# Two of four rounds per chunk weighted by ScalarE instead of VectorE in the four-head graph-attention layers

## The reference

```python
h = (h_in @ W).reshape(n, Hh, Cc)                # Hh = 4 heads, Cc = 64
alpha_s = jnp.sum(h * a_s, axis=-1)
alpha_d = jnp.sum(h * a_d, axis=-1)
e = jax.nn.leaky_relu(alpha_s[src] + alpha_d[dst], 0.2)
m = jax.lax.stop_gradient(jax.ops.segment_max(e, dst, num_segments=n))
ex = jnp.exp(e - m[dst])
alpha = ex / jax.ops.segment_sum(ex, dst, num_segments=n)[dst]
out = jax.ops.segment_sum(h[src] * alpha[:, :, None], dst, num_segments=n)
return out.reshape(n, Hh * Cc) + b
```

## Time and profile before

| What | us |
|---|---|
| Device time, median of 3 runs | 5079.66 |
| lowest and highest of the 3 | 5040.54, 5084.57 |
| Span of the profiled execution (first to last instruction) | 4873.4 |
| Around the span: the three runs less the span | 167 to 211, by the median 206.3 |
| Gathers of the first GAT layer, first start to last start | 3149.6 to about 3795 |
| Gathers of the second GAT layer | 3878.8 to 4526.0 |

### The profile page before, as it was taken

One profiled execution on the slowest core, in us unless ns is written; L12 is line 12 of the kernel. 1 busy time (PEld: TensorE's weight loads), 2 busy tenths in 40 slices (PEclk: granted clock), 3 DMA queues, 4 the chain that ended last, 5 costly groups with the idle time before them and its releaser, 6 DMA issues. The chain is left out here.

```text
span 4873.4 us, 62986 instructions
## 1 busy us (share of the span) xinstructions
PE 3036.0 (62%) x14559; PEld 2055.8 (42%) x14560; DVE 2601.7 (53%) x6219; ACT 1386.5 (28%) x3757; POOL 1985.7 (41%) x1861
## 2 busy tenths in 40 slices
PE   5498655597646455553669993355555455555289
PEld 3255113354213333332358993243333333343267
DVE  6655988655974678874331111344444444444421
ACT  0311431212421577773114441110110210110134
POOL 0000430001421777775002224377777477777300
PEclk9999875555777666776559996677776677767579
DMA  0132000222013677764012222244444244444200
GB/s 19 60 96 86 0 5 16 81 93 69 0 59 126 180 188 196 197 191 133 6 47 83 80 71 68 72 101 100 101 101 100 63 101 100 101 100 100 71 18 21
DMA packets 269152, 413.89 MB, mean 85 GB/s; under 512 B 98337, under 2 KB 192053, under 8 KB 268721
## 3 DMA queue, kind: packets, MB, share of 16 engines
q0 software_dynamic: 98256, 295.59, 23.1%
q1 hardware_dynamic: 169124, 116.08, 7.9%
q10 hardware_dynamic: 1728, 1.72, 0.1%
HBM read 373.41 MB, written 39.84 MB: 85 GB/s over the span
## 5 line engine op out<-in xcount | busy, mean ns | idle before, releaser
L1098 PE MATMUL gt_part<-gt_wv,all_ident 128*128 128x260 f32 x1920 | 733.3, 548 | 651.3 <-DVE gt_wv L1001 651.3
L918 POOL DMA_INDIRECT gt_rows<-h_rows,gt_idx x960 | 1003.3, 1045 | 314.6 <-issue 300.1
L1098 PEld LDWEIGHTS gt_part<-gt_wv,all_ident 128*128 128x128 f32 x1920 | 497.2, 271 | 887.5 <-DVE gt_wv L1001 786.3
L1098 PE MATMUL att_part<-att_wv,all_ident 128*128 128x264 f32 x960 | 386.1, 571 | 331.5 <-ACT att_wv L1080 210.0
L918 POOL DMA_INDIRECT att_rows<-kv_rows,att_idx x480 | 512.8, 1068 | 148.6 <-issue 145.0
L1098 PEld LDWEIGHTS att_part<-att_wv,all_ident 128*128 128x128 f32 x960 | 258.3, 282 | 459.5 <-DVE att_wv L1001 315.0
L1080 ACT ACTIVATE att_wv<-att_rows,att_wv 128x32 f32<-128x32 f32 x1920 | 419.9, 308 | 3.9
L1075 ACT ACTIVATE gt_wv<-gt_score 128x20 f32<-128x20 f32 x240 | 57.1, 238 | 1218.9 <-DVE gt_score L995 1218.9
L974 DVE TENSOR_TENSOR gt_prod<-gt_rows,gat_own 128x16 f32<-128x16 f32 x240 | 42.2, 176 | 574.8 <-SPq L896 551.2
L1001 DVE TENSOR_TENSOR gt_wv<-gt_rows,gt_wv 128x1024 f32<-128x1024 f32 x240 | 292.5, 1219 | 0.4 <-ACT gt_wv L1075 0.4
L608 POOL TENSOR_TENSOR ixcd_off_p<-ixcd_lane_e,all_iota_h 128x2048 f16<-128x2048 f16 x26 | 96.4, 3709 | 413.4 <-issue 304.7
(11 more groups left out here) (455 smaller groups left out, 5680.9 us busy)
## 6 DMA issues: line engine op xcount, KB each, us to landing
ixbs_parts_bc<-key_parts_s SPq DMA_DIRECT2D x28, 1024.0 KB, 6.2
ixbd_parts_bc<-key_parts_d SPq DMA_DIRECT2D x28, 1024.0 KB, 6.3
ex_w<-in_W SPq DMA_DIRECT2D x16, 1024.0 KB, 7.4
gt_rows<-h_rows,gt_idx POOLq DMA_INDIRECT x960, 2.9
att_rows<-kv_rows,att_idx POOLq DMA_INDIRECT x480, 3.8
y_rows<-ex_y POOLq DMA_DIRECT2D x55, 128.0 KB, 2.0
kv_rows<-qv_kv_all SPq DMA_DIRECT2D x5, 1300.0 KB, 6.5
gt_idx<-neighbours_d SPq DMA_DIRECT2D x240, 2.0 KB
```

The costliest lines, as they stand in the source:

```text
L918: pool.indirect_dma_start(out=rows[:, k, r, :], out_offset=None, in_=table, in_offset=bass.IndirectOffsetOnAxis(ap=idx[:, k, r:r + 1], axi ...
L1098: last = pe.matmul(part[:, k, 0:h * av], c.ident[:, :], wv[:, k, r, :, :].rearrange("p h f -> p (h f)"), start=(r == 0), stop=(r == ROUNDS ...
```

## The change

The number of rounds that ACT weights was half of the four in the eight-head layer and none in the GAT layers. It is now half in all three calls.

```diff
@@ attend, L848
-    act_rounds = ROUNDS // 2 if qk else 0
+    act_rounds = ROUNDS // 2
     dve_rounds = ROUNDS - act_rounds
```

## The result

| | Kernel before | Changed kernel |
|---|---|---|
| Device time, median | 5082.11 us (4 runs, 5040.54 to 5087.62) | 5137.28 us (4 runs, 5127.67 to 5143.28) |
| Ratio after / before | | 1.0119, 95% interval 1.008 to 1.0158 |
| Span of the profiled execution | 4873.4 us | 5141.7 us |

The change costs 1.2%; I had forecast 1.4% the other way. The span of the changed kernel stands 1.6 us under the time of its own run (5143.28), so next to nothing lies around a span. The 206 us that I had put "around the span" of the kernel before were inside the executions that were timed: its trace came from an execution of some 4875 us, the like of which none of the timed ones was.

The account below looks back on a forecast made before the run. POOL's gather issue was taken to bound the two GAT layers; 92.3 us of stretching gone less 23 back gains 69, so 5079.7 - 69 = 5010.7 us, with 8 in 10 between 4970 and 5052.

Parts of the forecast that it names:

- around the span: Time outside the profiled span, 206 us, taken as untouched, so the gain was subtracted from the median of timed runs.
- What bounds the kernel: In both GAT layers POOL's gather issue sets the pace, 5.01 us a chunk, stretched to 5.37 by L1001.
- The port rule: L1001 holds gathers 0.13 us after their start; halved to 0.68 us, it brings their mean from 1.045 to 0.97.
- The sum: Both GAT layers: 92.3 us of stretching gone, 23 back, 69 gained; span 4804, time 5010.7 us, 1.4% faster.
- the term for L1009: In GAT chunks k = 2 and 3, L1009 moves up and holds 65 of 120 gathers: 17 us back.
- So it stays hidden: The register load behind L1001 would still run under the shorter L1001 of 0.68 us.
- ACT under cover: ACT's eight activations, 2.2 us a GAT chunk, end 1.5 us before DVE's half and cost nothing in the loop.
- B: Rival: no change, 5080 us; stretched gathers only show another limit, such as the DMA engines; chance 0.13.
- C: Rival: ACT becomes the bound in the GAT layers, POOL waiting on it; 29 us more, 5109 us; chance 0.03.

Follow-up runs that it names:

- e11: The changed kernel again, its half written another way (same instructions), against the kernel before on a pausing machine: 5139.96 us, ratio 1.0132.
- e2: Kernel before with DVE weighting two of four GAT rounds and nobody the other two, quiet machine: 4804.16 us, ratio 0.9847.
- e3: Kernel before plus eight unused ACT activations per GAT chunk, DVE still weighting all four rounds, quiet machine: 4876.91 us, ratio 0.9998.
- e5: The changed kernel again, its half written another way (same instructions), against the kernel before on a quiet machine: 4793.54 us, ratio 0.983.
- e7: Changed kernel with ACT weighting three of four GAT rounds and DVE one: 5014.41 us in one run, kernel before 5085.53.
- e16: Changed kernel with ACT weighting three of four GAT rounds, measured again on a pausing machine: 5075.96 us, ratio 0.9946 to the kernel before.
- e19: Changed kernel plus a POOL fill of 128 columns ahead of each GAT chunk's third gather, pausing machine: 5172.28 us, ratio 1.0111 to the kernel before.

## Why the prediction was wrong

- **What bounds the kernel: wrong for the machine that was measured, and the step that failed.** "So the pace is set by how fast POOL issues gathers" holds for the execution that was profiled, and for no timed one. The evidence stood in the table: a span of 4873.4 beside runs of 5040 to 5085. I wrote "What lies around it is untouched, so against the median of the runs 5079.7 - 69", and took 206 us, 4% of the kernel, for overhead around a span without asking. After it, time and span differ by some 2 us in every run. What the runs showed in its place: the pauses take 200 us of the kernel before, POOL stands for slots, and what the port gives back (70 us, e11) is lost again in POOL's pauses (129 us more), by pauses that grow and by ACT's lost cover.
- **The port rule: right.** The gathers' mean was to be 0.97 us: 0.960 quiet, 0.968 and 0.969 pausing. L1001 took 0.684 (0.68 forecast). e2 gains by it alone.
- **The sum, on the machine that the trace came from: right, and 12 us short.** 69 forecast, 81 measured. Most of the difference is the term for L1009: 17 us forecast, 5.4 counted, since for k = 2 it starts 0.83 us after the start of L1001 and not 0.68, behind a register load that the shorter L1001 no longer hides. "So it stays hidden" was wrong there, to the good. For k = 0 and 1 L1009 did not move at all: it starts 1.5 to 1.6 us after the start of L1001 in both kernels, where no gather is near. L1001 itself kept 7.8 us, where I had 4.
- **ACT under cover: right on a quiet machine** (e3: 0.9998), wrong on a pausing one, where POOL waits 245 us for L1080 [e11]. "DVE stays the later of the two" and "The cover is 1.5 us" took for granted that DVE stands for the rows of the next chunk. It does in e5, and the cover is 1.5 us there; where POOL has run ahead the rows are there, and ACT ends 0.8 us behind DVE [e11].
- **Rivals.** B (no change, 5080) and C (ACT in POOL's way) each had a part of it: POOL's idle time does name ACT, as C's sign was to be, though an activation costs 0.25 us and not 0.60. None had pauses in it.

Open: what the pauses are, whether faster gathers cause their growth, and why three rounds on ACT have fewer of them than the even split. They occur in the three stretches with continuous gathers, not elsewhere, and in some jobs only. That the split with three rounds waits less is measured, in e7 and e16; its reason is not. Every run here has a recorded span, so none shows whether the pauses would be there without recording. Single runs lie some 40 us under the others in either condition (4836 beside 4873, 5035 beside 5081), also without a known reason.

## What to carry to other kernels

Before reading one row, hold the profiled span against the timed runs: where they are 4% apart, the trace shows an execution of another kind, and a bound read from it needs room for the engines that it shows idle. A faster bounding engine is worth only the slack behind it. The cover of an engine that works beside another is to be worked out once more for the case that the other does not wait. Of a split between engines try every ratio: three of four rounds on ACT beats the kernel before in both conditions (0.9849 and 0.9946), the even split in one only.

## What the runs showed of the hardware that I had not expected

- The instruction streams of SP and DVE, and in the eight-head layer that of ACT, can fall to about one instruction in 1.4 us (a register move of 29 ns took up to 1,387), in some jobs and not in others on the same chip; 200 us in 5,080 here. In the traces this comes only with continuous gathers of POOL, and is over within some 3 us of the last one.
- A gather issued by POOL is held by a DVE operation on two SBUF operands only if that started about 0.025 us or more ahead of the gather and still runs 0.13 us after the gather's start. The gather then ends 0.82 us after it: 229 stretches of the kernel before fit this within 0.03 us. The Trainium skill ("SBUF — State Buffer", section "SBUF: two separate sides") has such a lock held for whole instructions; the measurement decides, and halving one DVE instruction gave 77 us (e2).
- A POOL fill of 0.23 us between two gathers costs 0.08 us (e19).
